# Output products of linear-attention heads: four 32-column groups of the array, two heads to a group, in place of full-width blocks

## What is computed

```
h = layernorm(x) * (1 + ca) + sa
q, k, v = (h @ Wq, h @ Wk, h @ Wv)          # 16 heads of 16
gk = log_sigmoid(h @ Wgk1 @ Wgk2 + bgk2) / 16
state = state * exp(gk)[..., None] + v[..., None] * k[..., None, :]    # token by token
out_t = einsum('bhvk,bhk->bhv', state, q)
out = layernorm(out) * gamma + beta;  out = out * silu(h @ Wg);  x = x + ga * (out @ Wout)
...                                         # then layernorm, router, top 2 of 8 experts, gelu, sum
```

## Time and profile before

| | |
|---|---|
| median of three runs | 1197.76 us |
| lowest and highest | 1196.61 and 1199.06 us |
| span of the profiled execution | 1196.8 us |
| TensorE busy | 1042.1 us, 87% |
| VectorE busy | 823.3 us, 69% |
| GpSimd busy | 536.0 us, 45% |
| ScalarE busy | 490.5 us, 41% |
| mean granted TensorE clock | 0.930 |

### The profile page before, as it was taken

The page is one execution under the profiler, slowest core; times in us unless marked ns, Lnnn a source line. Parts: engine busy times, 40 slices in busy tenths (PEclk is TensorE's granted clock), DMA queues, the critical chain, the costliest instruction groups (busy, mean ns, idle before and its releaser), DMA issues.

```text
span 1196.8 us, 26755 instructions
## 1 busy us (share of the span) xinstructions
PE 1042.1 (87%) x6929; PEld 879.5 (73%) x6930; DVE 823.3 (69%) x1997; ACT 490.5 (41%) x1548; POOL 536.0 (45%) x525
## 2 busy tenths in 40 slices
PE   5899898888989889898884698989898998989896
PEld 4566665666666566665653698989898998989896
DVE  2577878878788787878866356566666566666653
ACT  1445444444444445454431342434333343334331
POOL 4454645556464554645552234334334343343432
PEclk9899999999999999999986798989899998989988
DMA  7701010111101011010001721212222222212221
GB/s 248 278 27 42 28 45 32 36 34 34 45 27 40 32 36 42 25 45 32 31 33 52 253 43 33 41 27 41 32 38 34 36 41 32 36 32 40 37 38 20
DMA packets 51451, 62.66 MB, mean 52 GB/s; under 512 B 6274, under 2 KB 46931, under 8 KB 51283
## 3 DMA queue, kind: packets, MB, share of 16 engines
q1 hardware_dynamic: 38546, 44.36, 11.7%
q0 software_dynamic: 12864, 17.83, 8.6%
HBM read 38.91 MB, written 23.27 MB: 52 GB/s over the span
## 4 chain that ended last, share of the span: by engine, by line
PE 60%; issue 17%; DVE 16%; DVEq 3%; DMA 1%; ACT 1%; SPq 1%; POOL 0%; ACTq 0%; POOLq 0%
PE p_a L1095 24%; PE p_qk L1095 9%; PE p_vg L1095 8%; PE p_z L1095 7%; PE p_cum L1095 6%; DVE hot L942 2%; PE p_tr L1095 1%; PE p_tr L1272 1%; PE p_o L1095 1%; PE p_qk L1114 1%; DVE w_r L919 1%; PE p_a L1114 1%; DVE w_hi L862 1%; DVE host_s L964 1%; DVE w_r L913 1%
## 5 line engine op out<-in xcount | busy, mean ns | idle before, releaser
L651 POOL DMA_INDIRECT out_dram<-x,tok x68 | 162.9, 2395 | 318.8 <-DVE x L1071 300.3
L589 POOL TENSOR_TENSOR w<-qkT_both,own 128x1024 f32<-128x1024 f32 x64 | 120.1, 1895 | 227.1 <-PE p_a L1095 214.5
L683 ACT ACTIVATE h2T<-p_tr,mods 128x128 f32<-128x128 f32 x200 | 80.4, 452 | 318.0 <-PE p_tr L1272 255.4
L1095 PE MATMUL p_a<-w,qkT_both 128*128 128x512 f32 x256 | 144.0, 645 | 32.7 <-DVE host_s L964 30.4
L1053 DVE COPY host_x<-w 128x1024 f32 x68 | 75.0, 1102 | 113.9 <-PE p_cum L1095 60.5
L1095 PE MATMUL p_a<-w_hi_r,host_s_r 128*128 x544 | 145.1, 299 | 2.3 <-DVE host_s_r L1078 2.3
L1095 PE MATMUL p_a<-w_r,host_s_r 128*128 x544 | 139.7, 289 | 0.0
L1095 PEld LDWEIGHTS p_o<-w_hi,w 128*128 128x128 f32 x1024 | 125.4, 193 | 15.3 <-issue 15.3
L1095 PE MATMUL p_o<-w_hi,w 128*128 128x128 f32 x1024 | 130.8, 276 | 0.0
L1095 PEld LDWEIGHTS p_a<-w_hi_r,host_s_r 128*128 128x128 f32 x544 | 102.2, 188 | 3.1 <-issue 2.8
L1095 PEld LDWEIGHTS p_a<-w_r,host_s_r 128*128 128x128 f32 x544 | 102.4, 188 | 0.1
(11 more groups left out here) (213 smaller groups left out, 2299.9 us busy)
## 6 DMA issues: line engine op xcount, KB each, us to landing
w<-in_L_ffn_W_dram SPq DMA_DIRECT2D x16, 1024.0 KB, 12.8
ln_host<-expert_rows SPq DMA_DIRECT2D x68, 136.0 KB
host_x<-in_L_attn_x_dram SPq DMA_DIRECT2D x64, 128.0 KB, 2.1
out_dram<-x SPq DMA_DIRECT2D x32, 128.0 KB, 1.7
w<-in_L_wmod_dram SPq DMA_DIRECT2D x1, 1536.0 KB, 7.1
expert_rows<-pad_rows SPq DMA_DIRECT2D x8, 136.0 KB, 1.7
out_dram<-x,tok POOLq DMA_INDIRECT x68, 4.7
b_all<-in_L_ffn_b_dram SPq DMA_DIRECT2D x1, 1024.0 KB, 8.2
```

The source lines that it names most:

```text
L589: last = nc.gpsimd.tensor_tensor(qbd[:, j, :, :], qkT[v][:, j, :].unsqueeze(1).to_broadcast([P, HB, P]), own[:].unsqueeze(2).to_broadcast( ...
L651: nc.gpsimd.indirect_dma_start(out=out, out_offset=bass.IndirectOffsetOnAxis(ap=tok[u][:, 0:1], axis=0), in_=y_out[u][:], in_offset=None, ...
L683: last = A.activation(dst[:, j, :], src[:, j * P:(j + 1) * P], ACT.Identity, scale=mods[:, which + 2 + j:which + 3 + j], bias=mods[:, whic ...
L1095: return nc.tensor.matmul(dst, lhsT, rhs, start=start, stop=stop, skip_group_check=True)
```

## The change

The eight heads of a half are taken as four pairs. A pair's output is 32 rows of `p_o`, so its products need 32 columns of the array: the columns of the pair's group m, which are also the partitions 32m to 32m + 31 of the output. The state product is cut into four in the same way. `vbd` shrinks from eight blocks with a step of 144 to four with a step of 48: v of the even head, 16 zeros, v of the odd head, so that a 32-column window at 0 gives the even head beside zeros and one at 16 gives zeros beside the odd head. The order is all four groups with their even heads, then all four with their odd ones. Score 3 is issued behind block 0 as a whole.

```diff
-    VSTEP = HB * HD + HD
+    PAIRS = HB // 2
+    VSTEP = 3 * HD
...
-        vbd = in_w1.take(KD, HB * VSTEP).rearrange("p (a c) -> p a c", a=KD)
+        vbd = in_w1.take(KD, PAIRS * VSTEP).rearrange("p (a c) -> p a c", a=KD)
...
                     for j in range(KD):
-                        last = nc.gpsimd.tensor_copy(
-                            vbd[:, j, :].rearrange("p (h c) -> p h c", c=VSTEP)[:, :, 0:HD],
-                            vn[v][:, j * P:(j + 1) * P].rearrange("p (h d) -> p h d", d=HD))
+                        for odd in range(2):
+                            last = nc.gpsimd.tensor_copy(
+                                vbd[:, j, :].rearrange("p (m c) -> p m c", c=VSTEP)[:, :, 2 * odd * HD:(2 * odd + 1) * HD],
+                                vn[v][:, j * P:(j + 1) * P].rearrange("p (m e d) -> p m e d", e=2, d=HD)[:, :, odd, :])
                     last.then_inc(vbd_ready, 1)
...
-                def output_of_block(j, midway=None):
-                    dst = p_o[:, j * P:(j + 1) * P]
-                    mm(dst, state[:, j * P:(j + 1) * P], qkT[u][:, j, :], True, False)
+                def output_of_block(j):
+                    W = P // PAIRS
+                    dst = [p_o[m * W:(m + 1) * W, j * P:(j + 1) * P] for m in range(PAIRS)]
+                    for m in range(PAIRS):
+                        mm(dst[m], state[:, j * P + m * W:j * P + (m + 1) * W], qkT[u][:, j, :], True, False)
                     pe.wait_ge(am_ready, 4 * s + 2 * j + 2)
-                    for h in range(HB):
-                        if midway and h == HB // 2:
-                            midway()
-                        last = mm(dst, vbd[:, j, h * P:(h + 1) * P],
-                                  am[:, 2 * j + h // 4, h % 4 * P:(h % 4 + 1) * P], False, h == HB - 1)
+                    for odd in range(2):
+                        for m in range(PAIRS):
+                            h = 2 * m + odd
+                            at = m * VSTEP + odd * HD
+                            last = mm(dst[m], vbd[:, j, at:at + W],
+                                      am[:, 2 * j + h // 4, h % 4 * P:(h % 4 + 1) * P], False, odd == 1)
                     return last
...
-                    output_of_block(0, midway=lambda: scores_of_heads(3))
+                    output_of_block(0)
+                    scores_of_heads(3)
```

## The result

| | before | after |
|---|---|---|
| median | 1197.18 us (1194.05 to 1199.06, 4 runs) | 1237.72 us (1237.26 to 1238.79, 4 runs) |
| span of the profiled execution | 1196.8 us | 1237.1 us (execution 1238.79 us) |
| mean granted clock | 0.930 | 0.876 |

The changed kernel is slower by 3.4%: ratio 1.0342, interval 1.0326 to 1.0359. Its time lies in the range of the prediction, 9.7 us above the number. The sum that led there was wrong in two of its three terms all the same, and the profile shows it at first sight.

What follows compares the result with a forecast made beforehand. The step's end was taken to hang on score 3's start, through GpSimd's masks and VectorE, with no p_o product waited for behind it. 1196.8 + 26.3 + 3.9, clock 0, made 1227.0, as a median 1228 us; range 1203 to 1246.

Steps and rivals of the forecast that it cites:

- The chain: From score 3 (last four heads' scores), GpSimd's masks, VectorE's small operations and the next score 0 follow, 7.84 us.
- Score 3 behind block 0, +26.3 us: TensorE, block 0: score 3 waits 2.05 us for twelve products in place of 1.11, 0.94 us later in 28 steps.
- If starts keep program order, the next group must wait for that second one: Block 0: each fp32 product is two instructions, so the next group starts beside the second; gives 2.05 us.
- the lower end, 0.84: Block 0 with all four groups side by side: three rounds of two instructions plus two width changes, 0.84 us.
- The gain bound of -6.2: Best case: score 3 starts when VectorE's mask of score 2 is done, 0.22 us earlier in 28 steps.
- The copies, +3.9: GpSimd: two vbd copies become four, 0.3 us more in each of 13 full-clock steps, +3.9 us.
- the upper bound of +6.8: Four vbd copies each as long as now: 0.52 us more in each of 13 full-clock steps, +6.8 us.
- The clock, 0: TensorE's share of half-clock stretches stays as it is: 0, bounds -18 (no slow steps) to +15.6 (all slow).
- By the value taken that time changes by 0.05 us a step: TensorE's standing still, 2.08 us a step, was taken to change by only 0.05 us, leaving the clock's share unchanged.
- all four at once, but TensorE waits itself cold: Groups overlap, TensorE stands still 3.2 us a step, all 28 steps turn slow at 1.2 us each: 1207; chance 0.10.

Runs made afterwards that it cites:

- e2: The kernel before with two added products of constants per step, one in each of TensorE's two waits, to hold the clock: 1177.24 us.
- e1: The changed kernel with three added products of constants per step, two ahead of the wait for chosen and one ahead of score 0: 1178.58 us.
- e5: The kernel before with score 3 moved behind the whole full-width block 0, and three added products per step to hold the clock: 1206.62 us.
- e9: e6 with the twelve products of a block written group by group in place of round by round: 1197.73 us.
- e3: The kernel before with only heads 0 and 4 multiplied in each half, full-width, 12 of 16 heads left out: 1245.28 us.
- e4: The kernel before with vbd filled by four copies of half the heads in place of two: 1200.11 us.
- e6: e1 with vbd laid out at a step of 32 per head, so that two copies fill it in place of four: 1172.62 us.
- e8: The changed kernel with one added product of constants per step, ahead of the wait for chosen: 1197.17 us.
- e7: The changed kernel with vbd filled by two copies in place of four and no added products: 1236.40 us.

## Why the prediction was right or wrong

*The chain: right.* It said that behind score 3 no `p_o` product is waited for and that the step's end hangs on score 3. 9.90 against 9.89 us from score 2 on, e2 against e1, and e5's 0.90 us for 0.89 show it. Its 7.84 us from score 3 to the next score 0 became 8.01 in the changed kernel, by the longer score 3 and by the copies.

*Score 3 behind block 0, +26.3 us: wrong, about -2.* The step that failed is "If starts keep program order, the next group must wait for that second one". The groups' instructions are interleaved (e9 shows starts out of the program's order; whether the compiler or the engine does it is not told apart), and the block takes 0.86 us, which is the lower end, 0.84, almost to the figure (score 3 starts no sooner in e3, where it waits for the mask). Score 3 then follows score 2 by 1.89 us in place of 2.05, and GpSimd starts 3.10 us behind score 2 (345.56 - 342.46) in place of 3.17: 28 x -0.07 = -2 us. The gain bound of -6.2 was too generous by two thirds: score 3 starts 0.06 us behind the end of the mask of score 2 (343.60 + 0.69 = 344.29), and it takes 1.13 us in place of 1.02, as it does in e3 (1.12), where it follows the wait for the mask and no width changes. The Trainium skill's rule of TensorE: Matmul & The Clock Gate, Part 3, that tiles of different groups overlap closely, agrees with the 0.62 us for sixteen instructions. Its other half, strict program order of the starts, does not fit e9 if the order is that in which the kernel is written; if the compiler changed the order, e9 says nothing about it.

*The copies, +3.9: right in size, right in part in place.* +3.2 in e4, by its medians; 0.24 us a step from e6 to e1 (18.19 to 18.43), 28 x 0.24 = +6.7 with all steps at the full clock, the upper bound of +6.8. A third of it lies at the end of the step, where the prediction had nothing (e4).

*The clock, 0: wrong, about +37.* The step that failed is "By the value taken that time changes by 0.05 us a step", which fell with the block; standing still went from 2.1 to 3.7 us. From the table, 28 x ((20.41 - 18.43) - (18.91 - 18.25)) = +37.0 us, and e1 over e2 is 28 x 0.18 = +5.0: together the 41.9 us by which the 28 steps grew (571.41 against 529.52). The +5.0 are the copies' +6.7 and score 3's -1.7. The rest of the spans' difference, -1.6 us, lies outside the steps.

*The rival that named it, "all four at once, but TensorE waits itself cold": the mechanism was right, its size was not.* All four groups ran at once, TensorE stood still longer (3.7 us, 3.2 said) and all steps but the first became slow. It priced a slow step at 1.2 us over a full one and came to 1207. A slow step is now 20.48 - 18.43 = 2.05 us over a full one, since the half clock lasts for 5.5 us of work and not 3.4: the price of a slow step was taken as fixed, and it is not. Nor does it simply grow with the standing still, as e8 shows (2.85 us, and 1.03 over a full step). The Trainium skill says in TensorE: Matmul & The Clock Gate, under "HAM oscillation — how this bites in real kernels", that idle gaps between bursts bring the lower clock back in every turn of a loop. This trace agrees: it came in every step, and in e1, which shortens the gaps to 0.86 and 0.27 us, in none.

*The number.* 1228 was near 1237.7 by luck: a delay that did not come (+26) stood where a clock that did (+37) should have stood. The sign and the range were met by luck too. The sum had the slowdown from a late score 3, and score 3 came earlier; what slowed the kernel is the term that the sum put at nothing.

## What to carry to other kernels

Ask what TensorE will do with the time that a change saves it: where another engine ends the step, it will stand still. Here the trace showed the clock falling in half of the steps already, and 2 us saved a step came back as 5.5 us of work at half clock. How much standing still is too much these runs do not give (e8 had 0.8 us more of it a step than the kernel before and no more slow steps), so it is to be tried. Such a trace has a gain that needs no saving at all: products of constants in the waits, into a bank that nobody reads at that time, took 1.5% off the kernel before and nearly 5% off the changed one. And fp32 products in four column groups overlapped here as well as their number promises, written round by round (0.86 us a block); written group by group they took 1.51.

## What the runs showed of the hardware that had not been expected

Four 32-column groups of plain fp32 products, two instructions each, lay side by side: 24 instructions in 0.86 us, where 0.84 was worked out for full overlap with two changes of width.

Three kernels with different work (after, e3, e7) settled on the same step of 20.48 us, though with the clock held the first and the last of them differ by 0.24 us (e1 and e6 are the same two with added products). Why it is that length was not settled by these runs.

TensorE's clock answered to one added product of constants per step, which shortened one wait from 2.57 to 1.72 us: 1237.7 us without it, 1197.2 with it.
